# Product with the values in two 64-row halves of the keys, in the unmasked attentions of a two-layer decoder

## The chip, the cores and the metric

The kernel is one launch on one core of a Trainium2 chip. The metric is the time of that launch on the device in microseconds. The kernel before takes 3052.56 us (median of three runs, 3050.74 to 3059.14).

## What is computed

Two decoder layers with the norm after each part, over x of 2048 positions by 256 channels, in float32. Each layer has a self-attention, a cross-attention over a context of 1601 positions, and a feed-forward part. All four attentions have 16 heads of 16 channels. Cut to what matters here:

```python
x = _layernorm(x + _L0_attn_ref(x, ...))             # causal, rotated and normed queries and keys
x = _layernorm(x + _L0_xattn_ref(x, ctx, ctx, mask)) # masked: the last keys are padding
x = _layernorm(x + _L0_ffn_ref(x, ...))              # linear, fp8
x = _layernorm(x + _L1_attn_ref(x, ...))             # causal, an MLP inside
x = _layernorm(x + _L1_xattn_ref(x, ctx, ctx, ...))  # no mask
x = _layernorm(x + _L1_ffn_ref(x, ...))              # 8 experts, 2 of them for each token, and a shared one
# in each attention, for each head:
scores = q @ k.T * scale
attn = softmax(scores)      # exp(s - rowmax) / sum
out = attn @ v
```

## The kernel before

One Python function, attention_phase, writes all four attentions. Heads are worked on in order. For a head the scores are made with the keys on the partitions: a **tile** is 128 keys (kt; 16 tiles in the self-attentions, 13 in the cross-attentions, the last of 65 keys), and a **step** is one tile by one half (1024) of the queries. A causal head has 24 steps, since tiles 8 to 15 need only the second half of the queries; a cross-attention head has 26.

In each step four kinds of work meet:

- **scores** (L569, two steps ahead): eight fp16 matmuls of 50 rows by 32 columns. Four go to one PSUM bank and use array rows 0 to 63, four to the next bank with rows 64 to 127 (the stack of queries and keys is there twice, once in each half of the partitions). The scores of step g+2 wait for the exponential of step g, since there are two pairs of score banks. In the first self-attention the diagonal is added by further matmuls (L575), in the masked cross-attention the mask by 128-row fp8 matmuls (L587).
- the **exponential** (L475, ScalarE), written as float32 with the keys on the partitions, into one of four slots. In the second self-attention GpSimd then clears what lies over the diagonal (L434, `select`).
- the **product** with the values (L609), once per tile when both halves of its queries are there: four float32 matmuls, one for each quarter of the columns, with all 128 keys as rows and 17 columns (16 channels, and ones for the sum of the weights). All tiles of a head add up in one PSUM bank (O_PS). Its end is told by `pv_done`. In a causal head tiles 0 to 3 take up to 512 queries of each quarter, 4 to 7 384, 8 to 11 256 and 12 to 15 128. Each float32 matmul stands in the trace as two.
- the **units** (L548): scores for a later head, with the queries on the partitions, of which VectorE takes the greatest of each row (L737, L727, L733), as the maximum for the softmax. A head has 64 units of 401 columns (cross) or 40 of 128 to 512 (causal). Each unit is four matmuls of 48 rows by 32 columns. Unit g uses rows 0 to 63 or 64 to 127 as g is even or odd. Three PSUM banks take turns: unit g waits until VectorE has read unit g-3 (`unit_used`).

TensorE's order in a step is written out by hand: the scores of step g+2, the first half of the step's units, the product if the step ends a tile, the other units. When a head is complete, ScalarE copies its bank out (`copy_out`, L448), after the exponential of the next head's first step, and the next head's first product waits for that (`o_copied`). Units belong to the head after this one, or the one after that, so the last head has none beside it.

Of the kernel before, what the change touches and what calls it, by code (L numbers as in the profile page):

```python
# [33 lines left out]
P = 128  # L34
# [3 lines left out]
H = 16  # L38
HD = D // H
# [3 lines left out]
CH = 512  # L43
# [59 lines left out]
def attention_phase(nc, e, keys, causal, masked, loads, query, key, value, ahead, projection, normed, eps, kept=None,  # L103
# [52 lines left out]
    with ExitStack() as held, phase(nc) as sem:  # L156
# [8 lines left out]
        s_ready, exp_done, pv_done = sem("s_ready"), sem("exp_done"), sem("pv_done")  # L165
        front_made, v_kept, o_copied = sem("front_made"), sem("v_kept"), sem("o_copied")
# [44 lines left out]
        MAX_STEPS = 5  # L211

# [35 lines left out]
        with nc.Block() as block:  # L248
# [194 lines left out]
            def _(act):  # L443
# [60 lines left out]
            def _(pe):  # L504
# [31 lines left out]
                def unit(h, u):  # L536

# [7 lines left out]
                    bank, first = e.ps[:, g % M_BANKS, :], g % 2 * ROWS  # L545
# [46 lines left out]
                def product(h, n):  # L592

                    kt, rows, _, _, _, _ = slots[n]
                    tile = h * nk + kt
                    pe.wait_ge(exp_done, h * ns + n + 1)
                    if select:
                        pe.wait_ge(selected, tile + 1)
                    if kt == 0 and h:
                        pe.wait_ge(o_copied, h)  # L600
                    if tile == 0 and v_bias:
                        pe.wait_ge(v_shifted, nk)
                    weights = e.prob[tile % P_SLOTS].rearrange("p (b j q) -> p b j q", j=4, q=P)
                    for j in range(4):
                        b0 = max(0, -(-(kt - j) // 4)) if causal else 0
                        if b0 == 4:
                            continue
                        end = kt == (12 + j if causal else nk - 1)
# [52 lines left out]
                for h in range(H):  # L661
                    for n in range(ns):
                        if n + 2 < ns:
                            scores(h, n + 2)
                        elif h + 1 < H:
                            scores(h + 1, n + 2 - ns)
                        turned = h + (1 if n <= turn else 2)
                        now = range(before[n], share[n]) if turned < H else range(0)
                        middle = -(-len(now) // 2)
                        for u in now[:middle]:  # L670
                            unit(turned, u)
                        if masked and h * ns + n + 2 < H * ns:
                            mask_scores(h + (n + 2) // ns, (n + 2) % ns)
                        if slots[n][5]:
                            product(h, n)
                        for u in now[middle:]:
                            unit(turned, u)
                pe.wait_ge(o_weights_in, 16 * NC)
# [1600 lines left out]
```

## Time and profile before

| | |
|---|---|
| time, median of 3 | 3052.56 us |
| the profiled execution's own time | 3052.74 us |
| its span | 3051.0 us |
| TensorE busy | 2817.6 us, 92% |
| VectorE busy | 2171.2 us, 71% |
| ScalarE busy | 1824.3 us, 60% |
| GpSimd busy | 542.7 us, 18% |
| mean granted TensorE clock | 0.952 |

The span has four stretches in which an attention's heads run: the first self-attention from 147 to 544 us, the masked cross-attention from 651 to 1313, the second self-attention from 1477 to 1865, the unmasked cross-attention from 2091 to 2681. TensorE's busy share counts any time in which a matmul is in the array, also one that uses few rows or columns, so it doesn't tell how much more the array could take. What an engine waits for has to be read inside a head.

### The profile page before, as it was taken

To read this page: it belongs to the slowest core of one execution; us is meant where nothing else is said; L and a number is where in the kernel's file an instruction comes from. 1 tells how busy PE (TensorE), PEld (TensorE's weight loads), DVE (VectorE), ACT (ScalarE), POOL (GpSimd) and SP (SyncE) were. 2 spreads that over 40 slices of the span, in tenths; PEclk is the share of its full clock that TensorE was granted. 3 is DMA by queue.
4 is the path that set the end of the run, shared out by engine and by line. 5 is a ranking of instruction groups with operands and counts; after the bars stand their busy time and mean duration, and the time that the engine had idled before them with its cause. 6 is when DMAs were issued, how large, how long until landed. Compare 5 with 4: busy or idle time off the path is not lost. (4 is left out here: it accounts for less than half of the span.)

```text
span 3051.0 us, 93944 instructions
## 1 busy us (share of the span) xinstructions
PE 2817.6 (92%) x39186; PEld 1046.2 (34%) x39187; DVE 2171.2 (71%) x6062; ACT 1824.3 (60%) x2158; POOL 542.7 (18%) x760
## 2 busy tenths in 40 slices
PE   4999999999999999967999998999999999899997
PEld 2522222522222222233222224652222222256664
DVE  7688986587878887565899993158888888652114
ACT  2388878436666666734588886234777777831222
POOL 0188870110000000001222113111000000002330
PEclk7899999979999999978899999997999999999999
DMA  3345541301110001102111112020111111111112
GB/s 98 111 130 131 135 111 35 118 18 25 25 26 25 17 24 26 36 20 76 33 47 43 42 45 83 1 74 23 39 52 52 52 53 32 35 58 62 44 43 86
DMA packets 120407, 166.79 MB, mean 55 GB/s; under 512 B 38227, under 2 KB 89310, under 8 KB 119984
## 3 DMA queue, kind: packets, MB, share of 16 engines
q1 hardware_dynamic: 102192, 117.21, 14.3%
q0 software_dynamic: 12320, 43.02, 4.6%
q8 instruction: 310, 5.08, 0.7%
q10 hardware_dynamic: 5472, 0.56, 0.2%
q14 instruction: 113, 0.93, 0.1%
HBM read 126.51 MB, written 26.72 MB: 50 GB/s over the span
## 5 line engine op out<-in xcount | busy, mean ns | idle before, releaser
L737 DVE TENSOR_REDUCE mpart<-ps 128x1 f32<-128x512 f32 (+2 forms) x1792 | 1014.2, 616 | 149.2 <-PE ps L548 148.1
L548 PE MATMUL ps<-stack 48*32 48x401 f16 (+5 forms) x13312 | 987.9, 355 | 55.3 <-DVE mpart L737 25.3
L475 ACT ACTIVATE xT<-ps,exp_scale 128x1024 f32<-128x1024 f32 (+3 forms) x800 | 794.6, 1028 | 284.6 <-PE ps L569 137.5
L475 ACT ACTIVATE cn<-ps,exp_scale 128x1024 f32<-128x1024 f32 (+4 forms) x800 | 743.1, 959 | 233.6 <-PE ps L569 119.7
L569 PE MATMUL ps<-stack 50*32 50x512 f16 (+3 forms) x11648 | 744.4, 377 | 56.2 <-ACT xT L475 42.3
L548 PEld LDWEIGHTS ps<-stack 48*32 48x32 f16 x13312 | 293.3, 91 | 1056.6 <-DVE mpart L737 562.8
L733 DVE CUSTOM_DVE_ANT_0 scrap<-ps,arena 128x401 bf16<-128x401 f32 (+1 forms) x1024 | 534.3, 574 | 128.0 <-PE ps L548 128.0
L609 PE MATMUL ps<-xT,vall 128*17 128x512 f32 (+4 forms) x3648 | 422.5, 524 | 2.2 <-POOL xT L434 1.4
L609 PE MATMUL ps<-cn,vall 128*17 128x512 f32 (+3 forms) x3392 | 412.9, 508 | 1.0 <-ACT cn L475 1.0
L569 PEld LDWEIGHTS ps<-stack 50*32 50x32 f16 x11648 | 194.6, 91 | 209.2 <-ACT xT L475 110.5
L727 DVE CUSTOM_DVE_ANT_0 scrap<-ps,scrap 128x128 bf16<-128x128 f32 (+3 forms) x512 | 247.6, 485 | 19.7 <-PE ps L548 15.1
L587 PE MATMUL ps<-arena,big 128*32 128x512 fp8e4 (+1 forms) x3264 | 256.8, 386 | 0.0
L1671 PE MATMUL ps<-arena,vall 128*128 x312 | 146.7, 593 | 0.6 <-ACT vall L1745 0.6
L1928 DVE TENSOR_TENSOR vall<-osb,ps 128x512 f32<-128x512 f32 x39 | 26.8, 688 | 146.0 <-PE ps L1671 146.0
L1761 ACT ACTIVATE osb<-ps 128x512 f32<-128x512 f32 x39 | 23.3, 597 | 169.8 <-PE ps L1671 169.8
L1152 POOL PARTITION_ALL_REDUCE small<-small x1 | 0.4, 371 | 687.4 <-issue 687.4
L609 PEld LDWEIGHTS ps<-xT,vall 128*17 128x17 f32 (+1 forms) x3648 | 71.5, 96 | 111.2 <-issue 46.1
L1574 POOL IOTA vall<- 128x16 f32 x1 | 0.2, 153 | 608.1 <-POOLq L248 608.1
L609 PEld LDWEIGHTS ps<-cn,vall 128*17 128x17 f32 (+1 forms) x3392 | 70.5, 96 | 109.0 <-issue 54.6
L422 POOL TENSOR_SCALAR arena<-wbuf 128x401 bf16<-128x401 int32 x64 | 101.2, 1581 | 6.3 <-DMA wbuf<-in_mask 2.5
L587 PEld LDWEIGHTS ps<-arena,big 128*32 128x32 bf16 (+1 forms) x3264 | 50.3, 94 | 120.8 <-issue 120.8
L733 DVE DVE_READ_ACCUMULATOR2_ANT mpart<- 128x1 f32 x1024 | 84.7, 83 | 0.0
(281 smaller groups left out, 2510.9 us busy)
## 6 DMA issues: line engine op xcount, KB each, us to landing
stack<-q_parts SPq DMA_DIRECT2D x384, 64.0 KB, 2.6
stack<-k_parts SPq DMA_DIRECT2D x192, 64.0 KB, 2.9
wbuf<-in_maskT POOLq DMA_DIRECT2D x24, 512.0 KB, 4.7
arena<-in_moe_w SPq DMA_DIRECT2D x19, 512.0 KB, 4.4
stack<-k_parts SPq DMA_DIRECT2D x192, 50.0 KB, 2.3
stack<-sums_inverse SPq DMA_DIRECT2D x16, 512.0 KB, 5.6
parts<-osb SPq DMA_DIRECT2D x240, 32.0 KB
wbuf<-in_mask POOLq DMA_DIRECT2D x16, 401.0 KB, 4.0
```

The lines of the kernel that those rows point to most:

```text
L422: chain.link(nc.gpsimd.tensor_scalar(e.mask_add[:, t, a:a + n], stage.bitcast(I32), 0.0, MASKED, ALU.is_equal, ALU.mult))
L475: nc.scalar.activation(e.prob[tile % P_SLOTS][0:rows, half * HALF + first:(half + 1) * HALF], S_PS(g)[0:rows, first:HALF], ACT.Exp, scale= ...
L548: last = nc.tensor.matmul(bank[quarter(j), 0:w], qs[b][rows, t * P + 32 * j:t * P + 32 * j + 32], ks[b][rows, a:a + w], start=True, stop=True)
L569: last = nc.tensor.matmul(S_PS(g)[quarter(j), lo:hi], ks[b][at:at + KM, kt * P + 32 * j:kt * P + 32 * j + 32], qs[b][at:at + KM, half * HA ...
L587: last = nc.tensor.matmul(S_PS(g)[quarter(j), lo:hi], e.big16[0:rows, quarter(j)], e.mask_one[0:rows, kt, half * HALF + lo:half * HALF + h ...
L609: last = nc.tensor.matmul(O_PS[quarter(j, HD + 1), b0 * P:CH], e.values[0:rows, kt, h, :], weights[0:rows, b0:4, j, :], start=(kt == 0), s ...
L727: nc.vector.tensor_tensor_reduce(out=e.scrap[:, t % 3, 0:w], in0=src, in1=e.scrap[:, 3, CH - w:CH], scale=1.0, scalar=-3.0e38, op0=ALU.add ...
L733: nc.vector.tensor_tensor_reduce(out=e.scrap[:, g % 4, 0:w], in0=src, in1=e.mask_add[:, t, a:a + w], scale=1.0, scalar=-3.0e38, op0=ALU.ad ...
L737: nc.vector.tensor_reduce(dst, src, AX, ALU.max).then_inc(unit_used, 1)
L1671: last = nc.tensor.matmul(bank, e.pair_xT[i % 2][:, c, :], w, start=(c == 0), stop=(c == NC - 1))
L1761: nc.scalar.activation(e.gated_s[i % 2], a_bank(i), ACT.Silu).then_inc(pair_silu, 1)
L1928: nc.vector.tensor_tensor(e.pair_h[i % 2], e.gated_s[i % 2], b_bank(i), ALU.mult).then_inc(pair_h, 1)
```

## The change

In the three attentions without a mask (both self-attentions and the second cross-attention) the product of a tile is issued twice: `upper_keys` for keys 0 to 63 of the tile, in the step that ends it (one step later where GpSimd clears the diagonal, `lag`), and `lower_keys` for keys 64 to 127 in the step after that. The units that follow an upper half in the step take array rows 64 to 127, those that follow a lower half rows 0 to 63. The lower half waits for the end of its upper half (`pv_half`), the upper half for the end of all lower halves before it (`pv_done`), since both add into the same bank. Units no longer stand between the scores and the first product half of a step. `copy_out` waits for the last lower half; it is where it was in ScalarE's order, or one exponential later with `lag`. The masked attention keeps its order.

```diff
@@ -163,6 +163,7 @@
+        pv_half = None if masked else sem("pv_half")
@@ -209,6 +210,7 @@
+        lag = 1 if select else 0
@@ -475,7 +477,7 @@
-                        if n == 0 and h:
+                        if n == lag and h:
                             copy_out(h - 1)
@@ -533,8 +535,7 @@
-                def unit(h, u):
-
+                def unit(h, u, group=None):
@@ -542,7 +543,7 @@
-                    bank, first = e.ps[:, g % M_BANKS, :], g % 2 * ROWS
+                    bank, first = e.ps[:, g % M_BANKS, :], (g % 2 if group is None else group) * ROWS
@@ -589,26 +590,48 @@
+                def product(h, kt, some, closes):
+
+                    tile, rows = h * nk + kt, k_tiles[kt][1]
+                    some = slice(some.start, min(some.stop, rows))
...
-                        last = nc.tensor.matmul(O_PS[quarter(j, HD + 1), b0 * P:CH], e.values[0:rows, kt, h, :],
-                                                weights[0:rows, b0:4, j, :], start=(kt == 0), stop=end)
-                    last.then_inc(pv_done, 1)
+                        end = closes and kt == (12 + j if causal else nk - 1)
+                        last = nc.tensor.matmul(O_PS[quarter(j, HD + 1), b0 * P:CH], e.values[some, kt, h, :],
+                                                weights[some, b0:4, j, :], start=(kt == 0 and some.start == 0), stop=end)
+                    return last
...
+                def upper_keys(g):
+
+                    h, kt = g // ns, slots[g % ns][0]
+                    pe.wait_ge(exp_done, g + 1)
+                    pe.wait_ge(pv_done, h * nk + kt)
+                    opened(h, kt)
+                    product(h, kt, slice(0, ROWS), False).then_inc(pv_half, 1)
+
+                def lower_keys(g):
+
+                    h, kt = g // ns, slots[g % ns][0]
+                    pe.wait_ge(pv_half, h * nk + kt + 1)
+                    product(h, kt, slice(ROWS, P), True).then_inc(pv_done, 1)
@@ -658,23 +681,45 @@
+                for g in range(H * ns):
+                    h, n = divmod(g, ns)
+                    if g + 2 < H * ns:
+                        scores(*divmod(g + 2, ns))
...
+                    else:
+                        closing, opening = ends_tile(g - lag - 1), ends_tile(g - lag)
+                        if not closing:
+                            middle = 0
+                        elif not opening:
+                            middle = len(now)
+                        if closing:
+                            lower_keys(g - lag - 1)
+                        for u in now[:middle]:
+                            unit(turned, u, 0)
+                        if opening:
+                            upper_keys(g - lag)
+                        for u in now[middle:]:
+                            unit(turned, u, 1)
```

TensorE's order in the unmasked cross-attention, two tiles of a head, before (L569 scores, L609 product, L548 units; a semaphore is printed under the name that its number had first):

```order
L569 MATMUL ps<-stack0_45156 32x512 [waits squared_49]
L569 MATMUL ps<-stack0_45156 32x512 x7
L548 MATMUL ps<-stack1_45156 32x401 [waits x_in3_49]
L548 MATMUL ps<-stack1_45156 32x401 x3
L609 MATMUL ps<-cn,vall 17x512 [waits squared_49]
L609 MATMUL ps<-cn,vall 17x512 x3
L548 MATMUL ps<-stack1_45156 32x398 [waits x_in3_49]
L548 MATMUL ps<-stack1_45156 32x398 x3
L569 MATMUL ps<-stack0_45156 32x512 [waits squared_49]
L569 MATMUL ps<-stack0_45156 32x512 x7
L548 MATMUL ps<-stack1_45156 32x401 [waits x_in3_49]
L548 MATMUL ps<-stack1_45156 32x401 x3
```

And the same attention after (L570 scores, L611 product half, L549 units; `rooted_49` is pv_half, `spread_49` pv_done, `squared_49` exp_done, `x_in3_49` unit_used):

```order
L570 MATMUL ps<-stack2_48036 32x512 [waits squared_49]
L570 MATMUL ps<-stack2_48036 32x512 x7
L611 MATMUL ps<-xT,vall 17x512 [waits rooted_49]
L611 MATMUL ps<-xT,vall 17x512 x3
L549 MATMUL ps<-stack0_48036 32x401 [waits x_in3_49]
L549 MATMUL ps<-stack0_48036 32x401 x3
L549 MATMUL ps<-stack0_48036 32x401 [waits x_in3_49]
L549 MATMUL ps<-stack0_48036 32x401 x3
L570 MATMUL ps<-stack2_48036 32x512 [waits squared_49]
L570 MATMUL ps<-stack2_48036 32x512 x7
L611 MATMUL ps<-xT,vall 17x512 [waits spread_49,squared_49]
L611 MATMUL ps<-xT,vall 17x512 x3
```

Every step now has a product half between its scores and its units, and each half waits for the half before it.

The late tiles of a causal head (second self-attention) before, tiles 12 to 14, one step each:

```order
L609 MATMUL ps<-xT,vall 17x128 [waits selected_32465,squared_49]
L609 MATMUL ps<-xT,vall 17x128 x3
L569 MATMUL ps<-stack_32466 32x128 [waits squared_49]
L569 MATMUL ps<-stack_32466 32x128 x3
L548 MATMUL ps<-stack_32466 32x512 [waits x_in3_49]
L548 MATMUL ps<-stack_32466 32x512 x3
L609 MATMUL ps<-xT,vall 17x128 [waits selected_32465,squared_49]
L609 MATMUL ps<-xT,vall 17x128 x2
```

And after, where both halves stand in one step:

```order
L570 MATMUL ps<-stack_33906 32x512 [waits squared_49,later_in_49]
L570 MATMUL ps<-stack_33906 32x512 x7
L611 MATMUL ps<-xT,vall 17x128 [waits rooted_49]
L611 MATMUL ps<-xT,vall 17x128 x3
L549 MATMUL ps<-stack_33906 32x128 [waits x_in3_49]
L549 MATMUL ps<-stack_33906 32x128 x3
L611 MATMUL ps<-xT,vall 17x128 [waits selected_33905,spread_49,squared_49]
L611 MATMUL ps<-xT,vall 17x128 x2
```

A tile's product here is one group of matmuls before, and after it is two groups in two steps, each of them behind a wait for the group before.

## Rows read from the trace of the kernel before

**Rows 1.** Stretches, engines' busy time, granted clock: three loops of heads, two heads, one clock dip.

```profile
core 0: us, PE busy (x) PEld busy (x) DVE busy (x) ACT busy (x) POOL busy (x), PEclk, DMA share, GB/s
147.20:543.90 396.70, 376.23 (x7713) 115.50 (x7710) 332.71 (x891) 319.94 (x397) 254.52 (x239) 0.98 0.41 107
1476.90:1864.80 387.90, 362.90 (x6714) 102.50 (x6711) 330.66 (x897) 317.11 (x398) 88.51 (x270) 0.99 0.17 41
2090.70:2681.20 590.50, 538.08 (x8630) 136.24 (x8627) 482.75 (x1017) 446.64 (x429) 8.96 (x14) 0.94 0.16 43
2164.60:2201.00 36.40, 33.01 (x573) 8.79 (x570) 32.58 (x70) 28.23 (x28) 0.00 (x0) 1.00 0.18 52
2201.00:2239.70 38.70, 35.60 (x572) 8.90 (x564) 32.61 (x69) 28.27 (x28) 0.00 (x0) 0.91 0.18 51
2202.30:2209.10 6.80, 6.49 (x64) 1.01 (x64) 4.05 (x8) 4.49 (x5) 0.00 (x0) 0.50 0.25 57
```

**Rows 2.** Waits in one head of the unmasked cross-attention (2164.6 to 2201 us): total, times, longest.

```profile
PEld ps L548 <- DVE mpart L737: 23.5, 38, 0.9
DVE mpart L737 <- PE ps L548: 3.7, 12, 0.7
```

**Rows 3.** Timeline, one tile of that attention: start, duration, engine, idle before.

```profile
2195.66 2.50 DVE L737 TENSOR_REDUCE mpart<-ps 128x1 f32<-128x401 f32 x5 [0.28 <-PE ps L548]
2196.78 0.35 PE L548 MATMUL ps<-stack 48*32 48x401 f16 x4
2197.06 1.05 PE L609 MATMUL ps<-xT,vall 128*17 128x512 f32 x8
2198.04 0.35 PE L548 MATMUL ps<-stack 48*32 48x401 f16 x4
2198.07 0.54 PE L569 MATMUL ps<-stack 50*32 50x512 f16 x8
2198.44 0.58 DVE L737 TENSOR_REDUCE mpart<-ps 128x1 f32<-128x401 f32 x1 [0.28 <-PE ps L548]
```

**Rows 4.** Timeline of the masked attention: from 64-row matmuls to 128-row ones and back.

```profile
903.27 0.34 PE L548 MATMUL ps<-stack 48*32 48x401 f16 x4
903.54 0.62 PE L587 MATMUL ps<-arena,big 128*32 128x512 fp8e4 x8
903.98 1.03 PE L609 MATMUL ps<-cn,vall 128*17 128x512 f32 x8
904.94 0.35 PE L548 MATMUL ps<-stack 48*32 48x398 f16 x4
```

**Rows 5.** Timeline of TensorE, second self-attention: products of three widths.

```profile
1609.86 0.84 PE L609 MATMUL ps<-xT,vall 128*17 128x384 f32 x8
...
1616.22 0.63 PE L609 MATMUL ps<-xT,vall 128*17 128x256 f32 x8
...
1620.29 0.41 PE L609 MATMUL ps<-xT,vall 128*17 128x128 f32 x8
```

**Rows 6.** Timeline, end of a head: last product, copy, exponential, next scores (2199 to 2203 us).

```profile
2199.83 1.05 PE L609 MATMUL ps<-cn,vall 65*17 65x512 f32 x8
2200.95 0.60 ACT L448 ACTIVATE osb<-ps 128x512 f32<-128x512 f32 x1 [1.15 <-PE ps L609]
2201.45 1.11 ACT L475 ACTIVATE cn<-ps,exp_scale 128x1024 f32<-128x1024 f32 x1
2202.61 0.12 PEld L569 LDWEIGHTS ps<-stack 50*32 50x32 f16 x8 [0.66 <-ACT cn L475]
2202.61 0.63 PE L569 MATMUL ps<-stack 50*32 50x512 f16 x8 [0.41 <-ACT cn L475]
```

**Rows 7.** Timeline, second self-attention: when ScalarE starts behind short scores.

```profile
1618.89 0.40 PE L548 MATMUL ps<-stack 48*32 48x512 f16 x4
1618.90 0.34 PE L569 MATMUL ps<-stack 50*32 50x384 f16 x4
...
1619.40 0.58 ACT L475 ACTIVATE xT<-ps,exp_scale 128x384 f32<-128x384 f32 x1 [0.38 <-PE ps L569]
1619.95 0.29 PE L569 MATMUL ps<-stack 50*32 50x256 f16 x4
1619.97 0.40 PE L548 MATMUL ps<-stack 48*32 48x512 f16 x4
...
1620.30 0.47 ACT L475 ACTIVATE cn<-ps,exp_scale 128x256 f32<-128x256 f32 x1 [0.32 <-PE ps L569]
```

More of the change, by code:

```diff
@@ L590, in mask_scores, with opened @@
                     last.then_inc(s_ready, 1)
[L592 to L596, printed above, removed]
+                def opened(h, kt):
                     if select:
-                        pe.wait_ge(selected, tile + 1)
+                        pe.wait_ge(selected, h * nk + kt + 1)
                     if kt == 0 and h:
                         pe.wait_ge(o_copied, h)
-                    if tile == 0 and v_bias:
+                    if kt == 0 and h == 0 and v_bias:
                         pe.wait_ge(v_shifted, nk)
+                def product(h, kt, some, closes):
+                    tile, rows = h * nk + kt, k_tiles[kt][1]
+                    some = slice(some.start, min(some.stop, rows))
                     weights = e.prob[tile % P_SLOTS].rearrange("p (b j q) -> p b j q", j=4, q=P)
@@ L607, in product, with whole @@
                             continue
-                        end = kt == (12 + j if causal else nk - 1)
-                        last = nc.tensor.matmul(O_PS[quarter(j, HD + 1), b0 * P:CH], e.values[0:rows, kt, h, :],
-                                                weights[0:rows, b0:4, j, :], start=(kt == 0), stop=end)
-                    last.then_inc(pv_done, 1)
+                        end = closes and kt == (12 + j if causal else nk - 1)
+                        last = nc.tensor.matmul(O_PS[quarter(j, HD + 1), b0 * P:CH], e.values[some, kt, h, :],
+                                                weights[some, b0:4, j, :], start=(kt == 0 and some.start == 0), stop=end)
+                    return last
+                def whole(g):
+                    h, kt = g // ns, slots[g % ns][0]
+                    pe.wait_ge(exp_done, g + 1)
+                    opened(h, kt)
+                    product(h, kt, slice(0, P), True).then_inc(pv_done, 1)
+                def upper_keys(g):
+                    h, kt = g // ns, slots[g % ns][0]
+                    pe.wait_ge(exp_done, g + 1)
+                    pe.wait_ge(pv_done, h * nk + kt)
+                    opened(h, kt)
+                    product(h, kt, slice(0, ROWS), False).then_inc(pv_half, 1)
+                def lower_keys(g):
+                    h, kt = g // ns, slots[g % ns][0]
+                    pe.wait_ge(pv_half, h * nk + kt + 1)
+                    product(h, kt, slice(ROWS, P), True).then_inc(pv_done, 1)
                 def open_totals(t):
@@ L660, in _, with ends_tile @@
                         mask_scores(0, n)
[L661 to L669, printed above, removed]
+                def ends_tile(g):
+                    return 0 <= g < H * ns and slots[g % ns][5]
@@ L670, in _ @@
+                for g in range(H * ns):
+                    h, n = divmod(g, ns)
+                    if g + 2 < H * ns:
+                        scores(*divmod(g + 2, ns))
+                    turned = h + (1 if n <= turn else 2)
+                    now = range(before[n], share[n]) if turned < H else range(0)
+                    middle = -(-len(now) // 2)
+                    if masked:
                         for u in now[:middle]:
                             unit(turned, u)
-                        if masked and h * ns + n + 2 < H * ns:
-                            mask_scores(h + (n + 2) // ns, (n + 2) % ns)
@@ L674, in _ @@
-                        if slots[n][5]:
-                            product(h, n)
+                        if g + 2 < H * ns:
+                            mask_scores(*divmod(g + 2, ns))
+                        if ends_tile(g):
+                            whole(g)
                         for u in now[middle:]:
                             unit(turned, u)
+                    else:
[12 more added lines that the diff above has]
+                            unit(turned, u, 1)
@@ L678, in _ @@
+                if not masked:
+                    for g in range(H * ns, H * ns + lag + 1):
+                        if ends_tile(g - lag - 1):
+                            lower_keys(g - lag - 1)
+                        if ends_tile(g - lag):
+                            upper_keys(g - lag)
                 pe.wait_ge(o_weights_in, 16 * NC)
```

## The prediction

> **What bounds the kernel now.** I began with the busy time by stretches [rows 1]. The three loops that the change touches take 396.7, 387.9 and 590.5 us, so 24.8, 24.2 and 36.9 us for a head. In none is an engine full: VectorE is busy 84, 85 and 82% of them, ScalarE 81, 82 and 76%. So the time is set by how the engines wait for each other, and I read the waits of one head of the cross-attention next [rows 2]. TensorE's weight loads for the units wait 23.5 us of 36.4 for VectorE to free a bank, and VectorE waits 12 times, 3.7 us together, for a unit. Each is held up by the other.
>
> The timeline shows the place [rows 3]. VectorE reduces five units in 2.50 us, which is (2.50 - 0.57)/4 = 0.48 us each with 0.57 for a single one. A unit is issued at 2196.78, the product begins at 2197.06, the next unit can only begin at 2198.04, and VectorE, out of work, begins it at 2198.44 after 0.28 us of idling. The product has the array to itself for 0.98 us, and once per tile VectorE runs dry. A head's 64 units at 0.48 us and some 0.5 us of small operations need 31.2 us of VectorE, against 36.4 us for the head: this is what the change can reach at most.
>
> **What is removed.** Two things. First, the change between matmuls of 64 rows and of 128. In the masked attention [rows 4] a unit of 401 columns, 0.17 us at 2.4 GHz, starts at 903.27 and the 128-row matmuls only at 903.54, 0.10 us after it. The product starts at 903.98, 0.44 us after the two rounds of 512 columns (0.21 us each) began, so there the change of type costs nothing. After the change all matmuls of these loops have up to 64 rows, and about 0.2 us per tile goes. Second, units and a product half lie in different rows and can run at once. No row shows a float32 matmul beside an fp16 one; scores and units of different rows do overlap, as the unit at 2198.04 and the scores at 2198.07 [rows 3]. I take it that the product does too, and price the other case below.
>
> **What is added: a half costs as much as the whole.** A matmul's time goes by its columns, not its rows: the product over 65 keys takes 1.05 us like that over 128 [rows 3, 6]. So each tile has two groups of 1.05 us (512 queries), 0.84 (384), 0.63 (256) or 0.41 (128) [rows 3, 5].
>
> **What is added: one chain through all halves.** An upper half waits for the end of the lower half before it, and that for its own upper half. The wait is for the recorded end, and the engine that waits starts 0.05 to 0.07 us after it: ScalarE at 2200.95 behind a product ended at 2200.88, TensorE at 2202.61 behind an exponential ended at 2202.56 [rows 6]. TensorE waits for no matmul of its own in the trace of before; I take 0.06 us for it, between a bound of 0 and one of 0.11 (which rows 7 show, below). What can't overtake stands behind each of these waits in TensorE's order: the units, then the next scores.
>
> Causal heads, four tiles of each width: 2 x 4 x (1.05 + 0.84 + 0.63 + 0.41) = 23.4 us, and 32 waits of 0.06 = 1.9, so 25.3 us. That is already over the 24.2 to 24.8 of now, where a tile's product was made once with units and scores between.
>
> **Between heads the chain breaks.** The last lower half must end before copy_out, and ScalarE takes the copy before the next exponential. From there: copy 0.50 us until the next exponential starts, exponential 1.11, wake of TensorE 0.05, scores about 0.23 before the first upper half, together 1.9 us [rows 6]. Before, this cost TensorE 0.66 us of waiting in a cross-attention head [rows 6]. Now the last half starts one step later, behind scores that already wait for the exponential in front of the copy, so ScalarE has nothing to do for the whole of it.
>
> A causal head then takes at least 25.3 + 1.9 = 27.2 us. Both loops: 16 x 27.2 = 435.2, less 396.7 and 387.9: **+38.5 and +47.3 us**. VectorE's work (332.7/16 = 20.8 us a head) hides under it, but not evenly: units go by the width of a step, 40 x 2048/17408 = 4.7 in the two steps of tile 0, at 20.8/40 = 0.52 us 2.45 us, against 2 x 1.11 of the chain. Tiles 0 and 1 so add 0.3 us to a head: **+10 us** for 32 heads.
>
> **The unmasked cross-attention.** Its chain is 26 x 1.11 + 1.9 = 30.8 us, just under VectorE's 31.2; VectorE stays ahead in cost. But a second thing keeps it from running at its own pace. Scores of 384 columns issued 0.01 us after a unit of 512 in other rows are recorded as ended at 1619.24; ScalarE starts them at 1619.40, 0.16 us later, which is 0.11 us after the end of the longer unit at 1619.29. Where the scores come first, at 1619.95 for 0.29 us, ScalarE starts 0.06 us after their end [rows 7]. So the end of a short matmul is told only after the end of longer ones issued before it. A unit issued beside a product half then reaches VectorE no sooner than the half's end plus 0.11 us.
>
> With that: VectorE needs the next unit 1.66 - 0.28 = 1.38 us after the last one was issued [rows 3]. After the change the half begins about 0.24 us after that unit (scores between), ends at 1.29, and the unit is reported at 1.40. In a step with two units the half begins later still, since the chain needs 1.11 us for a step and two units only 0.97; that gives some 0.14 us of idling. Over 26 steps, half of them with two units, 2.1 us. At the head's end VectorE has three banks, 1.45 us, to bridge nearly 2.5 us (1.9 and the reporting of the next unit): 0.9 us. So 31.2 + 2.1 + 0.9 = 34.2 us for a head, where it was 36.4: -2.2 us, for the 14 heads with units beside them -31. The last two run at the chain's 30.8 us with a loss of about 1 each: **-29 us**.
>
> The Trainium skill, page "TensorE: Matmul & The Clock Gate", Part 3 under "What overlaps and what doesn't", calls matmuls strictly in order at their start and at their end, which speaks against this change. The trace agrees for what other engines are told, by the 0.11 us above, though the recorded ends themselves are out of order. By the recorded ends alone a unit would be reported 0.35 us after its issue and a cross-attention head would come to 31.2 + 0.9 us, another -29 us for the whole.
>
> **The sum**, against the profiled execution's 3052.7 us (the median of the runs is 3052.6): 3052.7 + 38.5 + 47.3 + 10 - 29 = 3119.5. I say 3119. The masked attention keeps its order, and 0.
>
> **The granted clock.** In the cross-attention every other head has a dip to 1.2 GHz of 6.8 us just after the head's end, where TensorE had waited, and is 38.7 us long rather than 36.4 [rows 1]: 2.3 us. I keep the dips as they are. The wait at a head's end grows to over 1 us in all three loops. With a dip at each of the 32 causal heads, 2.3 us each, +74; with none left, -18.
>
> **Rivals.**
> - *The chain is short* (faster). If a half could start on the end of the last column and not of the recorded matmul, a half would cost 0.98 - 0.10 = 0.88 us for 512 columns [rows 3], some 0.17 less than 1.05 each, and no 0.06. Then a causal head is 25.3 + 1.9 - 32 x 0.23 = 19.8, VectorE's 20.8 and 1.5 of idling decide at 22.3, and both loops win 71 us (713.6 for 784.6); cross heads at 32.1 win another 58. That is about 2925. The point from which the whole is faster: a causal head under 25.4 us with the cross-attention as forecast, so a wait cheaper by 0.06 us for each half, or half of that with less idling in the cross-attention. For it: the recorded ends are modelled. Against it: ScalarE and VectorE start just 0.05 to 0.1 us after these ends everywhere.
> - *The gain and the chain cancel.* The cross-attention comes down to VectorE's 31.2 (14 heads, -73, and +2 for the last two) and loses its dips (-18), causal heads take no more than the chain (+86): 3050. The neighbouring case within 0.3% is this with some idling.
> - *More clock dips*: the forecast with dips at most heads: 3165 to 3195.
> - *No overlap of a float32 half with fp16 units.* Then 1.11 us of every half stands alone, and units (0.18 us each in one row group) and scores (0.23) add: a cross tile 2 x (1.11 + 0.23 + 0.44) = 3.6 us for 2.8, +166 us in 16 heads; causal heads 27.2 + 40 x 0.2 = 35, +335 for 32. About 3550. It would speak for it that no row has the pair; against it, types follow each other without a gap in [rows 4].
>
> **How the numbers follow.** Forecast 0.60, more dips 0.12, no overlap 0.05: slower 0.77. The case that cancels 0.10, of which 0.06 within 0.3% (about what a measurement of this kernel can tell from no change) and 0.04 below. The short chain 0.13. So faster 0.17, same 0.06, slower 0.77. The forecast's own bounds: waits of 0 or 0.11 us (-61 or +51), idling in the cross-attention of none or all (-43 or +29), seldom together; the 8 in 10 reach from the cancelling case to many dips, 3040 to 3185.
>
> **What would show it.** In the profile after: the two causal loops at 27 to 28 us a head, each product half starting 0.05 to 0.1 us after the end of the one before; ScalarE waiting over 1 us for the product before each copy; VectorE's idle time up in the causal loops, down in the cross-attention, whose heads take 34 to 35 us; units starting beside halves, while VectorE starts them only at the half's end. Causal heads under 25 us, or units reported in the middle of a half, would make it wrong.

## The result and the profile after

The changed kernel takes 3357.6 us (median of four) against 3055.9 for the kernel before: 1.0984 times as long, 95% interval 1.0955 to 1.1013. The forecast was 3119, range 3040 to 3185. The direction was right and the size was not: 302 us instead of 66. One of the four runs took 3467.6 us at a lower granted clock, and the ratio leaves it out. The profiled execution took 3353.95 us, its span is 3352.2.

The page of the profile after, busy times, granted clock in 40 slices, and the group in which VectorE takes the maxima (busy, mean ns, idle before):

```profile
PE 3108.6 (93%) x44563; PEld 1190.3 (36%) x44563; DVE 2196.4 (66%) x6062; ACT 1855.2 (55%) x2158; POOL 543.1 (16%) x760
PEclk7996978788999999987999998798889999969999
L782 DVE TENSOR_REDUCE mpart<-ps 128x1 f32<-128x512 f32 (+2 forms) x1792 | 1028.6, 618 | 276.5 <-PE ps L549 266.3
```

TensorE is busy 291 us longer, VectorE and ScalarE 25 and 31 us. In this group VectorE waits for units 266 us, where it was 148.

The stretches, which answer to [rows 1]: the three loops of heads, the last head of the second and of the third loop (they have no units), a long head of the first loop, an ordinary one of the second, and an undisturbed one of the third:

```profile
146.10:690.60 544.50, 497.70 (x9581) 173.29 (x9566) 343.25 (x894) 329.34 (x398) 255.77 (x241) 0.82 0.30 78
1624.40:2130.60 506.20, 466.18 (x8565) 144.33 (x8554) 339.15 (x895) 322.82 (x398) 88.23 (x270) 0.90 0.13 32
2356.20:2978.90 622.70, 596.80 (x10305) 176.25 (x10290) 490.34 (x1019) 463.61 (x431) 9.65 (x15) 0.90 0.15 41
2084.90:2130.60 45.70, 42.68 (x361) 9.98 (x362) 3.31 (x3) 19.37 (x25) 4.83 (x15) 0.50 0.13 30
2923.40:2978.90 55.50, 53.50 (x389) 9.01 (x390) 3.31 (x3) 28.73 (x28) 0.00 (x0) 0.51 0.10 25
305.70:345.80 40.10, 37.04 (x620) 13.00 (x616) 23.37 (x61) 21.04 (x26) 33.10 (x33) 0.66 0.44 111
1745.80:1776.50 30.70, 28.14 (x556) 8.99 (x552) 22.75 (x62) 20.31 (x26) 6.11 (x18) 0.94 0.13 35
2546.20:2582.40 36.20, 34.44 (x672) 11.10 (x668) 33.11 (x69) 29.05 (x27) 0.00 (x0) 1.00 0.19 57
```

The loops are 147.8, 118.3 and 32.2 us longer; the masked attention takes the same. Read the third number from the end of each row: the granted clock was 0.98, 0.99 and 0.94 before [rows 1], and is 0.82, 0.90 and 0.90 now. A causal head without a long dip takes 30.7 us, one with a long dip 40.1. The last heads, which took 21.4 (second loop) and 28.1 us (third) before, run at half the clock (1.2 GHz) and take 45.1 and 54.9 from one copy to the next. An undisturbed cross head is where it was, 36.2 for 36.4.

The chain of halves, in tiles 8 to 11 of a causal head (the answer to [rows 5]; TensorE's weight loads and matmuls):

```profile
1769.03 0.12 PEld L611 LDWEIGHTS ps<-xT,vall 64*17 64x17 f32 x7 [0.55 <-PE ps L611]
1769.03 0.41 PE L611 MATMUL ps<-xT,vall 64*17 64x128 f32 x4
1769.06 0.40 PE L549 MATMUL ps<-stack 48*32 48x512 f16 x4
1769.15 0.50 PE L611 MATMUL ps<-xT,vall 64*17 64x128 f32 x4
1769.75 0.14 PEld L611 LDWEIGHTS ps<-cn,vall 64*17 64x17 f32 x6 [0.59 <-issue]
1770.47 0.12 PEld L611 LDWEIGHTS ps<-cn,vall 64*17 64x17 f32 x7 [0.56 <-PE ps L611]
...
1771.92 0.40 PE L549 MATMUL ps<-stack 48*32 48x512 f16 x4
1772.01 0.50 PE L611 MATMUL ps<-cn,vall 64*17 64x128 f32 x4
1772.61 0.69 DVE L782 TENSOR_REDUCE mpart<-ps 128x1 f32<-128x512 f32 x1 [0.72 <-PE ps L549]
```

Three things can be read here. The unit at 1769.06 runs beside the product half: float32 and fp16 overlap in different rows. And one half starts 0.72 us after the other, weight loads of the halves waiting 0.55 us for TensorE's own matmuls. The half's last matmuls end at 1769.65, the next load is at 1769.75. And VectorE, idle for 0.72 us, takes the unit of 1771.92 only at 1772.61: its matmuls are recorded as ended at 1772.32, but VectorE starts 0.10 us after the end of the half that was issued before it (1772.51), as [rows 7] had it.

ScalarE is drawn in, which the prediction did not have. In the head of the second loop from 1745.8 us it waits six times, 5.3 us together, for a product half to free one of its four slots; in a head of that loop before the change it never did. Whether this wait costs anything beyond the chain itself, no run shows.

A tile of the undisturbed cross head (the answer to [rows 3]):

```profile
2559.92 0.60 PE L611 MATMUL ps<-xT,vall 64*17 64x512 f32 x4
...
2561.14 0.62 PE L611 MATMUL ps<-cn,vall 64*17 64x512 f32 x4
2561.22 0.35 PE L549 MATMUL ps<-stack 48*32 48x398 f16 x4
2561.57 0.61 PE L611 MATMUL ps<-cn,vall 64*17 64x512 f32 x4
2561.71 0.83 PE L549 MATMUL ps<-stack 48*32 48x401 f16 x8
2562.20 0.10 PEld L549 LDWEIGHTS ps<-stack 48*32 48x32 f16 x4 [0.38 <-DVE mpart L782]
2562.21 0.56 PE L570 MATMUL ps<-stack 50*32 50x512 f16 x8
2562.30 0.57 DVE L782 TENSOR_REDUCE mpart<-ps 128x1 f32<-128x398 f32 x1 [0.16 <-PE ps L549]
2562.60 0.60 PE L611 MATMUL ps<-cn,vall 64*17 64x512 f32 x4
```

The halves start 1.22 us apart in a step with two units and 1.46 in one with three. In the longer one the half has ended at 2562.18, but the scores, behind the third unit and its wait for a bank, come only at 2562.21, and the next half behind them at 2562.60.

The end of a cross head (the answer to [rows 6]):

```profile
2581.33 1.05 PE L611 MATMUL ps<-xT,vall 1*17 1x512 f32 x8
2582.31 0.69 PE L549 MATMUL ps<-stack 48*32 48x401 f16 x12
2582.45 0.60 ACT L450 ACTIVATE osb<-ps 128x512 f32<-128x512 f32 x1 [2.55 <-PE ps L611]
2584.10 0.63 PE L570 MATMUL ps<-stack 50*32 50x512 f16 x8 [1.10 <-ACT cn L477]
```

ScalarE waits 2.55 us for the last half (1.15 before), TensorE then 1.10 us for the exponential behind the copy (0.41). The last half here is that of a tile of 65 keys, so it has one key, and still costs 1.05 us; nothing runs beside it: the next unit begins 0.98 us after it starts, as behind the 128-row product [rows 3].

### The profile page after: what moved, and what is told of

Its sections match the earlier page's. It is cut to its first block and busy times, and to the rows that moved or that the text cites. A ratio compares the mean times of both kernels' runs of the same rounds, so it can differ in the third digit from the quotient of the medians.

```text
span 3352.2 us, 105146 instructions
## 1 busy us (share of the span) xinstructions
PE 3108.6 (93%) x44563; PEld 1190.3 (36%) x44563; DVE 2196.4 (66%) x6062; ACT 1855.2 (55%) x2158; POOL 543.1 (16%) x760
## 5 line engine op out<-in xcount | busy, mean ns | idle before, releaser
L549 PE MATMUL ps<-stack 48*32 48x401 f16 (+5 forms) x13312 | 1137.1, 368 | 26.1 <-DVE mpart L782 9.6
L570 PE MATMUL ps<-stack 50*32 50x512 f16 (+3 forms) x11648 | 920.0, 399 | 60.3 <-ACT xT L477 47.4
L477 ACT ACTIVATE cn<-ps,exp_scale 128x1024 f32<-128x1024 f32 (+4 forms) x800 | 763.4, 961 | 370.6 <-PE ps L570 177.2
L611 PE MATMUL ps<-xT,vall 64*17 64x512 f32 (+5 forms) x6464 | 807.2, 560 | 20.3 <-PE ps L611 5.7
L611 PE MATMUL ps<-cn,vall 64*17 64x512 f32 (+6 forms) x5952 | 762.1, 522 | 23.3 <-PE ps L611 5.8
L549 PEld LDWEIGHTS ps<-stack 48*32 48x32 f16 x13312 | 310.3, 91 | 832.5 <-DVE mpart L782 435.8
L570 PEld LDWEIGHTS ps<-stack 50*32 50x32 f16 x11648 | 221.9, 93 | 182.8 <-ACT xT L477 86.0
L611 PEld LDWEIGHTS ps<-xT,vall 64*17 64x17 f32 (+2 forms) x6464 | 141.5, 96 | 294.7 <-PE ps L611 100.6
L611 PEld LDWEIGHTS ps<-cn,vall 64*17 64x17 f32 (+3 forms) x5952 | 135.8, 95 | 307.6 <-PE ps L611 107.5
L841 DVE RECIPROCAL osb<-ps 128x128 f32<-128x128 f32 x16 | 15.2, 952 | 118.1 <-PE ps L730 118.1
```

The costliest lines, as they stand in the source:

```text
L549: last = nc.tensor.matmul(bank[quarter(j), 0:w], qs[b][rows, t * P + 32 * j:t * P + 32 * j + 32], ks[b][rows, a:a + w], start=True, stop=True)
L570: last = nc.tensor.matmul(S_PS(g)[quarter(j), lo:hi], ks[b][at:at + KM, kt * P + 32 * j:kt * P + 32 * j + 32], qs[b][at:at + KM, half * HA ...
```

## The experiments

Three theories for the 302 us. **Chain**: the halves, each waiting for the one before, set the pace. **Clock**: the time went to a lower granted clock. **Bank**: units wait in TensorE's order for VectorE to free a bank, and hold up what stands behind. The head times below are from one copy of a head's bank to the next. "Undisturbed" is a head in which the clock did not fall.

**Two unit banks, with the chain and without.** Both run with `M_BANKS = 3 if masked else 2`; in the second the lower half also adds into the bank that is left over, so that no half waits for another, and the sum over the lower keys is left out of the output (lines left out at ...):

```diff
-                    pe.wait_ge(pv_done, h * nk + kt)
...
-                    product(h, kt, slice(0, ROWS), False).then_inc(pv_half, 1)
+                    product(h, kt, slice(0, ROWS), True).then_inc(pv_half, 1)
...
-                    pe.wait_ge(pv_half, h * nk + kt + 1)
-                    product(h, kt, slice(ROWS, P), True).then_inc(pv_done, 1)
+                    product(h, kt, slice(ROWS, P), True, e.ps[:, 2, :]).then_inc(pv_done, 1)
```

Expected of the first: 

> The changed kernel with two PSUM banks for the units instead of three in the unmasked attentions, so that a third is left over; the waits between the product halves are kept. It is the control for the next kernel. Chain theory (each half waits for the reported end of the half before, and that sets a causal head): causal heads stay near 30 to 31 us, cross heads get longer since VectorE has one bank less ahead. Bank theory (units wait in TensorE's order for a bank that VectorE frees late, and hold up scores and halves behind them): all three loops get clearly longer, causal heads too, by 2 us or more. Clock theory (the time went to a lower granted clock): longer as far as the granted clock falls.

Expected of the second: 

> As the control with two unit banks, but the lower half adds into the bank that is left over and no half waits for another (the sum over the lower keys is not added to the output: it is left out). The same matmuls, units and banks. Chain theory: causal heads fall by the 32 handoffs of 0.07 to 0.1 us and the streaming that can now overlap, to VectorE's and ScalarE's pace, 24 to 27 us instead of over 30, so over 100 us less for the whole than the control. Bank theory: less than 30 us between the two. Clock theory: no change but for dips.

Measured: 4414.6 us (1.444, 1.438 to 1.450) and 3477.2 us (1.138, 1.135 to 1.141). The third loop of the first, and the loops and the last causal head of the second:

```profile
2937.00:4041.60 1104.60, 975.89 (x10305) 242.72 (x10290) 517.14 (x1018) 464.81 (x430) 8.99 (x14) 0.50 0.09 23
```

```profile
1666.50:2138.90 472.40, 419.43 (x8570) 166.51 (x8555) 345.96 (x895) 326.39 (x397) 87.83 (x270) 0.92 0.14 35
2385.50:3113.40 727.90, 643.77 (x10306) 202.00 (x10291) 509.77 (x1018) 458.49 (x430) 8.94 (x14) 0.87 0.13 35
2116.90:2138.90 22.00, 19.92 (x362) 7.52 (x363) 3.41 (x3) 17.95 (x24) 6.27 (x15) 0.85 0.25 62
```

The control fell to half the clock and stayed there, 48 to 52 us for a causal head and 70.4 for a cross head, so no theory had its number and the difference of 937 us holds both causes. Where banks don't matter, in the last heads, the same matmuls without the chain take 20.1, 22.0 and 28.7 us in the three loops. In the changed kernel and in the control it is 46.1, 45.1 and 54.9. Chain and clock go together here too: without the chain the clock was 0.85 in the second of these heads, with it 0.50. An undisturbed causal head of the second loop takes 28.6 us without the chain, above the 24 to 27 expected. With two banks most cross heads without the chain still take 44 to 50 us, against 36.3 for an undisturbed one with three banks and the chain: the third bank is worth about 8 us of a head.

**Matmuls that nobody reads, in the last heads.**

Only the call is shown:

```diff
+                        for u in filling:
+                            filler(u, 0 if closing and not opening else 1)
```

> The changed kernel, with matmuls of a unit's shape that nobody reads, in the places of the units, in the last head of the three unmasked attentions, where there are no units. Clock theory: in the changed kernel these last heads ran at a granted clock of 0.50 for their whole length (46.7, 45.7 and 55.5 us); with the array kept busier the clock comes back to 1.0 for most of them, they take 28 to 33 us, and the whole is 40 to 65 us faster, though it does more work. Chain theory alone (halves as long as they are, the clock no cause): no change, or some us slower.

Measured: 3327.9 us (1.0896, 1.0855 to 1.0936), about 30 us less than the changed kernel. The three last heads:

```profile
641.20:672.50 31.30, 28.43 (x577) 10.79 (x578) 3.31 (x3) 19.49 (x25) 0.00 (x0) 0.91 0.18 44
2082.30:2111.90 29.60, 27.26 (x501) 9.14 (x502) 3.41 (x3) 18.14 (x23) 6.31 (x15) 0.92 0.20 47
2920.80:2954.60 33.80, 32.37 (x638) 10.71 (x635) 3.31 (x3) 27.93 (x27) 0.00 (x0) 0.95 0.18 42
```

They get 15, 16 and 21 us shorter with more work in them, and the clock is back. The whole gained less than these 51: apart from its last head the second loop was 14 us longer, with a first head at half the clock, and the third 16 us, with more dips. The clock is a cause. And at 0.91 to 0.95 of the clock these heads are 11, 8 and 5 us longer than those without the chain (20.1, 22.0, 28.7). That is what the chain costs them at most, since the matmuls that nobody reads are in the one and not in the other.

**Each unit's matmuls twice, in the causal attentions.**

```diff
-                    for j in range(4):
+                    for j in list(range(4)) * (2 if causal and group is not None else 1):
```

> The changed kernel with the four matmuls of each unit issued twice in the two causal attentions (the second time with the same result), in the rows that the product half beside them leaves free. Clock theory: the long dips of the first self-attention (24 to 27 us at 1.2 GHz in two of four heads, heads of 39 to 40 us beside 30.6) go, and its loop gets shorter by 40 us or more, although there is more work. Chain theory alone: heads without a dip don't change or get up to 3 us longer, since a unit's second pass of 0.2 us stands ahead of the next scores; in all slower, by up to 60 us.

Measured: 3363.7 us (1.1006, 1.0976 to 1.1036). The two causal loops, and a head of the second:

```profile
146.80:674.60 527.80, 488.73 (x11909) 204.61 (x11894) 347.31 (x894) 330.77 (x398) 255.62 (x241) 0.93 0.31 81
1613.40:2122.00 508.60, 480.76 (x10897) 169.68 (x10886) 346.18 (x897) 324.77 (x398) 87.39 (x270) 0.94 0.14 33
1766.40:1796.90 30.50, 28.82 (x715) 10.64 (x712) 23.22 (x61) 20.43 (x26) 6.02 (x19) 1.00 0.12 31
```

The heads of 39 to 40 us in the first loop are gone (31.2 to 33.1 now), the loop is 17 us shorter with 2300 more matmuls, less than the 40 expected. The second loop stays where it was though its clock rose from 0.90 to 0.94. So with each unit twice a causal head takes 30.5 us at the full clock. With units once there is an undisturbed one in the first loop of the kernel with the filled last heads: 29.8 us. The doubling and the short dips each cost a head under 1 us. The third loop, untouched here, was 15 us longer by more dips, which is how much such dips vary.

**The change in the cross-attention alone.** The causal attentions take the whole product, in the order of before.

> The change in the unmasked cross-attention alone; the causal attentions keep the whole product in the order of before. The third loop took 622.6 us after the change and 590.5 before, the two others 265 us more. If the loops don't bear on each other: 3052 + 32 = 3085 us. Chain theory: an undisturbed cross head is level with before (36.3), and all of the loss is the last head, 54.9 us at half the clock for 28.1, and one or two more dips.

Measured: 3101.3 us (1.0169, 1.0151 to 1.0187). The causal loops are back at 394.9 and 391.7 us, the third loop takes 634, with heads of 38.6 to 39.7 us in turn, a single undisturbed one of 36.3 and a last one of 54.9. An undisturbed head is level with before, so this loop's loss of 43 us comes with the clock (0.87 for 0.94), more of it than expected; the whole was expected at 3085.

**The whole product one step later.** In the kernel before:

```diff
-                        if slots[n][5]:
-                            product(h, n)
+                        late = h * ns + n - (0 if masked else 1)
+                        if late >= 0 and slots[late % ns][5]:
+                            product(late // ns, late % ns)
...
+                if not masked:
+                    product(H - 1, ns - 1)
```

> The kernel before, with the whole product one step later in the three unmasked attentions (128 rows, once per tile, units around it), so that only the delay of the last product, and with it of the copy, is in it. Border theory (the copy's later start costs ScalarE and so TensorE 1 to 2 us at each of 45 head ends): 30 to 70 us slower than before. If the border is cheap because banks bridge it: within 15 us of before.

Measured: 3211.5 us (1.0515, 1.0499 to 1.0532), 160 us above before, where 30 to 70 were expected. The first two loops:

```profile
148.10:633.90 485.80, 450.08 (x7694) 123.71 (x7691) 335.51 (x889) 318.00 (x397) 253.35 (x238) 0.82 0.33 87
1566.80:2009.70 442.90, 391.97 (x6698) 104.79 (x6695) 337.13 (x894) 316.62 (x396) 87.67 (x270) 0.94 0.15 36
```

With no half in it, the delay alone brings an undisturbed causal head from 24.4 to 27.2 us, and draws the clock of the first loop down to 0.82, as in the changed kernel. Of these 2.8 us the head's end has about 1.1: the copy starts 2.15 us after the start of the last exponential of the head, 1.01 before. The rest lies inside the head.

**The upper half alone, and the same with each unit twice.** The product over keys 64 to 127 is left out, `lower_keys` is not called, and `lag` is 0, so the second self-attention has its upper half one step earlier (lines left out at ...):

```diff
-                    pe.wait_ge(pv_done, h * nk + kt)
...
-                    product(h, kt, slice(0, ROWS), False).then_inc(pv_half, 1)
+                    product(h, kt, slice(0, ROWS), True).then_inc(pv_done, 1)
```

> The changed kernel with the upper half alone: keys 64 to 127 of each tile are left out of the product, so there is one 64-row group per tile and no half waits for another; the units' rows stay as in the change. What the 64 rows bring if a half did not cost a whole: chain theory expects cross heads at 32 to 34 us and causal heads at 21.5 to 23.5, the whole at 2930 to 3000 us, with the last heads at the full clock. Clock theory (64-row work lowers the clock by itself): dips as in the changed kernel, 3100 or more.

> The kernel with the upper half alone (keys 64 to 127 left out of the product), with each unit's matmuls issued twice in the three unmasked attentions. The kernel without the doubling had a granted clock of 0.50 in the whole of its second and third loop (34.1 and 50.5 us a head, 3466 us in all). Clock theory: too little goes on in the array for the full clock, and the doubled units bring it back: cross heads at 32 to 36 us, causal ones at 24 to 27, the whole at 2950 to 3100 us, 350 us or more faster with more matmuls. If the heads are long because of the order of 64-row work itself: no change or slower.

Measured: 3466.5 us (1.136, 1.133 to 1.139), and with the doubled units 3124.7 us (1.021, 1.017 to 1.025). The second and third loop of the one, then of the other:

```profile
1547.10:2081.00 533.90, 492.04 (x6729) 201.40 (x6710) 341.78 (x899) 330.12 (x398) 87.38 (x271) 0.50 0.13 30
2306.40:3089.70 783.30, 749.21 (x8641) 221.45 (x8626) 483.31 (x1019) 463.65 (x430) 9.61 (x15) 0.50 0.12 32
```

```profile
1502.00:1925.70 423.70, 395.53 (x9065) 182.46 (x9050) 333.33 (x899) 324.56 (x398) 87.72 (x271) 0.92 0.16 39
2151.20:2765.20 614.00, 569.99 (x12385) 226.37 (x12374) 485.93 (x1019) 461.65 (x431) 9.52 (x14) 0.91 0.15 42
```

Half the product's work, and the kernel is slower than with all of it, where the chain theory expected 2930 to 3000 us: the clock stays at 1.2 GHz for the whole of two loops, although TensorE is busy 92 and 96% of them. With 3700 more matmuls in the third loop the clock is back and the loop is 169 us shorter. A cross head is then 37.1 us and a causal one 25.7 to 26.0, above the 32 to 36 and within the 24 to 27 expected; the doubled units cost something themselves, which these runs don't separate.

**The last tile of each head whole, in its old step.** The copy is also back in its old place.

```diff
-                    return 0 <= g < H * ns and slots[g % ns][5]
+                    return 0 <= g < H * ns and slots[g % ns][5] and (masked or g % ns != ns - 1)
...
+                        if n == ns - 1:
+                            last_tile(g)
```

> The changed kernel with the last tile of each head as one 128-row product in the step where it was before, so that the copy starts where it did before; all other tiles stay in halves that wait for each other. Border theory (the late copy costs 2.8 us of a causal head and about 2 of a cross head, as the product one step later did in the kernel before, and the TensorE idling there draws the clock down): causal heads fall from 30.6 to 26.5 to 28.5 us, most short dips go, the whole falls by 100 to 160 us. Chain theory alone: one tile less in the chain, 1 us a head, 30 to 50 us. The last heads stay at half the clock in both.

Measured: 3284.2 us (1.0744, 1.0682 to 1.0807), 73 us less than the changed kernel. A cross head falls from 36.3 to 35.1 us and that loop loses most of its dips ahead of the last head (583.8 us, less than before the change); an undisturbed causal head still takes 29.3. The second loop got 19 us longer (525.2 us at a clock of 0.85), so the dips moved, too. The end of the head thus costs at most 1.2 us of a head of the changed kernel and some of its dips, less than the 2 to 4 that the border theory said. The chain theory had 1 us as well, for the one half less, and the run doesn't tell the two apart. Most of a causal head's added length lies elsewhere.

**The product cut by queries.** 128 rows as before; each step takes the columns of its own half of the queries, as soon as their exponential is there:

```diff
-                        if slots[n][5]:
+                        if not masked or slots[n][5]:
                             product(h, n)
...
+                        if split:
+                            b0 = max(b0, 2 * half)
+                        b1 = 2 * half + 2 if split else 4
-                                                weights[0:rows, b0:4, j, :], start=(kt == 0), stop=end)
-                    last.then_inc(pv_done, 1)
+                                                weights[0:rows, b0:b1, j, :],
+                                                start=(kt == 0 and not (split and half)), stop=end and closes)
+                    if closes:
+                        last.then_inc(pv_done, 1)
```

> The kernel before, with the product cut by queries instead of keys in the three unmasked attentions: 128 rows as before, but at the end of each step only the columns of that step's half of the queries (up to 256 of each quarter), so nothing is computed twice and no half waits for another. Idle theory (VectorE runs dry because the array is shut for 0.98 us, longer than its banks bridge): a block of 0.55 us is bridged, VectorE's idling of 0.28 us per tile goes, cross heads fall from 36.4 to 33 to 35 us; causal heads gain less, tiles 8 to 15 being as before; two more drains of 0.1 us per tile are paid. In all 20 to 50 us faster than before. If the drains and more instructions outweigh it: 0 to 20 us slower.

> The product cut by queries (128 rows, at the end of each step the columns of its half) in all four attentions, the masked one too. In the three others it took 2968.6 us, with cross heads of 32.1 us and causal heads as before. In the masked attention VectorE idles 8.3 us of a head of 42.2, and TensorE comes to the product from other 128-row matmuls, so the cut adds no change of rows there in the step that had a product and one in no other. Idle theory: masked heads fall by 1 to 3 us, the whole to 2920 to 2955 us. If TensorE is full there (it waits only 7.5 us for weights): no change, 2960 to 2975.

Measured: **2968.6 us** (0.9733, 0.9720 to 0.9746), and with the masked attention too **2948.5 us** (0.9650, 0.9636 to 0.9663). Both beat the kernel before and the changed one. The third loop of the first, the masked loop of the second, and the timeline of a cross head (2250 us) of the first:

```profile
2086.50:2595.80 509.30, 503.15 (x10314) 149.49 (x10307) 473.13 (x1019) 454.87 (x431) 10.18 (x15) 0.99 0.19 50
```

```profile
644.60:1288.90 644.30, 643.53 (x13570) 217.43 (x13563) 513.53 (x1963) 467.75 (x430) 9.05 (x14) 1.00 0.10 25
```

```profile
2249.55 2.60 DVE L742 TENSOR_REDUCE mpart<-ps 128x1 f32<-128x398 f32 x5
2250.03 0.63 PE L612 MATMUL ps<-xT,vall 128*17 128x256 f32 x8
2250.58 0.35 PE L548 MATMUL ps<-stack 48*32 48x401 f16 x4
```

The array is shut for 0.55 us at a time (0.98 in [rows 3]) and VectorE runs on through it. Cross heads take 32.1 us, the dips are gone (0.99 for 0.94), the loop is 81 us shorter. That is more than the 33 to 35 us a head and the 20 to 50 us in all that were expected, and the gain that the change was after. VectorE is busy 31.8 of the 32.1 us. The causal loops don't move (393.0 and 389.9 us), less than the small gain expected. In the masked attention a head goes from 42.2 to 40.8 us, within the 1 to 3 expected.

## Why the prediction was right in its direction and wrong in its size

**Right: a half costs a whole, and they overlap with units.** The half of 256 columns was put at 0.63 + 0.06 and came 0.72 us after the one before. The half with one key takes 1.05 us.

**Right in kind, too cheap: the chain.** The step that failed is "32 waits of 0.06 = 1.9" in the causal heads. The sum had 27.5 us for such a head, with 1.9 at the border and 0.3 for tiles 0 and 1; measured were 29.8 us in the one undisturbed head with filled last heads, 29.3 with the last tile whole and 30.5 with the units twice. In the head of 29.8 us (from 176.4 us on) the halves add up to 23.2 us, as priced (23.4). But the 31 gaps between the recorded end of one half and the start of the next add up to 4.7 us, not 1.9. Three halves of its tiles 8 to 11, the product being L621 in this kernel:

```profile
197.44 0.41 PE L621 MATMUL ps<-cn,vall 64*17 64x128 f32 x4 [0.17 <-PE ps L621]
197.55 0.51 PE L621 MATMUL ps<-cn,vall 64*17 64x128 f32 x4
198.13 0.41 PE L621 MATMUL ps<-cn,vall 64*17 64x128 f32 x4
198.25 0.50 PE L621 MATMUL ps<-cn,vall 64*17 64x128 f32 x4
198.91 0.41 PE L621 MATMUL ps<-cn,vall 64*17 64x128 f32 x4 [0.16 <-ACT xT L477]
```

The lower half at 198.13 starts 0.07 us after its upper half has ended, and so it is for most lower halves of the head (0.06 to 0.10). The upper halves at 197.44 and 198.91 start 0.17 and 0.16 us after the lower half before them, and 13 of 15 lie at 0.15 to 0.19 (all of them at 0.10 to 0.14 in the second loop's heads that I read). Why these take longer stays open. The rest are a few long gaps, 0.78 and 0.39 us in this head and 0.92 once in each of those: I let the scores stream inside the handoff of two halves, and where a unit waits for its bank ahead of them, they and the half behind them come late, as in the tile of the cross head above (2562.21, then 2562.60, for a half ended at 2562.18). Over 32 heads those 2 to 3 us are 60 to 95 us. This is read from the traces; no kernel took one of these waits alone away.

**Wrong: the cross-attention's -29.** The forecast had 34.2 us for an undisturbed head, measured 36.2, 28 us in 14 heads. VectorE idles 3.1 us of it, which is the forecast's 2.1 + 0.9. The term that was mis-sized is VectorE's own time: 31.2 us, at 0.48 for every unit, where it is busy 33.1. [rows 1] already had 32.58 in a head. A unit that VectorE takes after idling costs 0.57 [rows 3], and it still idles about once a tile; with almost no idling, in the product cut by queries, it is busy 31.8. That cut shows that the gain was there to be had, without a chain.

**The end of the head.** The wait before the copy was forecast as over 1 us and was 2.55, and TensorE's idling behind it 1.10 us. The kernel with the last tile whole puts its price at 1.2 us a head at most; in the kernel before, a delay of the same kind cost a causal head 2.8 us, 1.1 of them at the head's end.

**Wrong above all: "I keep the dips as they are".** The three loops had 17, 5 and 67 us at 1.2 GHz before and 200, 103 and 124 after, 338 us more. Long heads against ordinary ones in the first loop (40.1 at a clock of 0.66, 30.7 at about 0.94) say that 0.4 of such a time is lost, so about 130 us. That is an estimate. The rest of the 300, about 170, stands against the 67 of the forecast's sum, and is these 67 with the 28 of the cross heads and some 75 of the causal ones. I had the rival with more dips, and priced it at +74 on the grounds of [rows 1], one dip of 6.8 us and 2.3 us lost for each. What I did not see is that the clock can stay down: 24 to 27 us in four heads of the first loop, 45 to 55 us in each last head, and with less to do beside the halves for hundreds of us.

**Rivals.** No overlap: refuted by the unit at 1769.06. The short chain: refuted by the start of each half behind the recorded end. The gain and the chain cancel: refuted, with cross heads at 36.2 us where this case needs 31.2. More dips, at 0.12, was the case that came, beyond its own price of 3165 to 3195.

## What to carry to other kernels

Before work is split to let it overlap, ask along which axis a piece gets cheaper: these matmuls cost by columns, so halves by rows doubled the product, and halves by columns did not. Two pieces that add into one bank from different rows are a chain, and each link costs the recorded end of a matmul plus a wake (0.06 to 0.19 us here), for itself and all that is queued behind. And TensorE's clock is part of the sum: where the trace of a change shows stretches at 0.50 with TensorE busy for nearly all of them, as here in every last head, price such stretches at 1.2 GHz too.

## What the runs showed of the hardware that I had not expected

- The granted clock can be 0.50 through whole loops with TensorE busy 92 to 96% of the time. In the kernel with the upper half alone it was, for 534 and 783 us; with each unit's matmuls issued twice it was 0.92 and 0.91, and the kernel 342 us faster.
- With two unit banks instead of three and the chain of halves the clock was 0.50 in three loops, and the kernel took 4415 us.
- A 64-row float32 matmul does run beside fp16 matmuls in the other 64 rows. The one-key half does not: the next unit starts 0.98 us after it.
- VectorE, idle, starts on a unit 0.3 us after its recorded end where a longer product half was issued before it (1772.32 and 1772.61).
